# A graph layer with a gated expert mix on one core: the row fix by one-hot products, the last sums stored ahead of the output loads, two of seven tiles mixed on TensorE

## The reference, cut to what matters

```python
x = x + relu(ln(x) @ W + segment_sum((ln(x) @ M)[src], dst))      # 6250 nodes x 256, 200000 edges
xn = ln(x)
h = (xn @ W_gat).reshape(M, 4, 4)                                 # 4 heads x 4 experts
e = leaky_relu(a_src[src] + a_dst[dst], 0.2)                      # 131072 edges, and one loop per node
ee = exp(e - segment_max(e, dst)[dst])
alpha = ee / (segment_sum(ee, dst)[dst] + 1e-16)
scores = layernorm(segment_sum(h[src] * alpha, dst) + b_gat).mean(heads)
w = softmax(top2(scores))                                         # per node, over 4 experts
x = x + sum_e w[:, e] * (gelu(xn @ W1[e] + b1[e]) @ W2[e] + b2[e])
```

## Time and profile before

| | us |
|---|---|
| median of 3 runs | 3240.63 |
| lowest, highest | 3239.18, 3240.84 |
| the profiled execution's own time | 3242.23 |
| its span | 3240.9 |

### The profile page before, as it was taken

How to read it: one execution, slowest core, us unless ns; L and a number is a source line. 1 busy time by engine, 2 the same in 40 slices (tenths; PEclk the granted TensorE clock), 3 DMA queues, 4 the chain that set the end, 5 groups by cost and what they waited for, 6 DMA issues and landing times.

```text
span 3240.9 us, 41199 instructions
## 1 busy us (share of the span) xinstructions
PE 2411.0 (74%) x13096; PEld 1894.9 (58%) x13096; DVE 2192.3 (68%) x5126; ACT 543.2 (17%) x924; POOL 2331.4 (72%) x2315
## 2 busy tenths in 40 slices
PE   1466878878778888788888888886888888888300
PEld 0344555556556555566666666664788887888200
DVE  6488777678685656565556555553588888888568
ACT  4000212112123333211111111111000000000012
POOL 3777777777777777777777777774777777777073
PEclk9777999889889989899999999898999999999655
DMA  8876777667767777777777777774122122211518
GB/s 277 297 226 218 221 224 226 216 214 230 218 208 243 239 223 238 223 223 236 232 247 246 239 235 238 234 237 131 26 62 62 39 61 62 55 44 44 192 43 270
DMA packets 470542, 599.63 MB, mean 185 GB/s; under 512 B 66293, under 2 KB 409270, under 8 KB 468278
## 3 DMA queue, kind: packets, MB, share of 16 engines
q1 hardware_dynamic: 372310, 375.12, 34.9%
q0 software_dynamic: 97568, 220.03, 24.6%
q10 hardware_dynamic: 448, 1.85, 0.2%
HBM read 312.22 MB, written 286.19 MB: 185 GB/s over the span
## 4 chain that ended last, share of the span: by engine, by line
PE 32%; DVE 16%; DMA 9%; issue 6%; POOL 5%; SPq 3%; ACT 1%; DVEq 0%; POOLq 0%; ACTq 0%
PE wide L1266 9%; PE wide L1368 9%; PE wide L1324 5%; PE wide L1314 5%; DMA run_d<-ring 4%; DVE g L871 2%; DMA fetched<-x_d 2%; DVE ring L746 2%; DVE low_hot L788 2%; DVE comb L995 2%; DVE picked L799 2%; PE wide L1283 2%; POOL ring L1438 1%; POOL start_d L1454 1%; DMA ring<-xn_d,srci 1%
## 5 line engine op out<-in xcount | busy, mean ns | idle before, releaser
L1438 POOL DMA_INDIRECT ring<-xn_d,srci x1611 | 1623.4, 1008 | 516.7 <-issue 443.6
L746 DVE SCALAR_TENSOR_TENSOR ring<-ring,same_v,wide 128x256 f32<-128x256 f32 x1610 | 770.6, 479 | 694.8 <-PE wide L1266 588.0
L1266 PE MATMUL wide<-ring,one_hot 128*128 128x256 f32 x3222 | 916.8, 421 | 164.5 <-DVE ring L746 95.1
L1266 PEld LDWEIGHTS wide<-ring,one_hot 128*128 128x128 f32 x3222 | 652.7, 211 | 377.8 <-DVE ring L746 132.6
L1368 PE MATMUL wide<-tab_parts,low_hot 128*128 128x208 bf16 x6144 | 599.9, 263 | 120.2 <-DVE low_hot L788 120.2
L1368 PEld LDWEIGHTS wide<-tab_parts,low_hot 128*128 128x128 bf16 x6144 | 576.4, 102 | 145.5 <-DVE low_hot L788 128.4
L1465 POOL DMA_INDIRECT g<-tab_d,srt x512 | 547.2, 1069 | 156.0 <-issue 154.2
L1324 PE MATMUL wide<-w2s,hh 128*128 128x256 f32 x1568 | 390.1, 394 | 2.3 <-DVE yo L724 2.3
L1314 PE MATMUL wide<-xt,w1s 128*128 128x512 f32 (+1 forms) x832 | 390.8, 594 | 0.8 <-DVE feat L714 0.8
L1324 PEld LDWEIGHTS wide<-w2s,hh 128*128 128x128 f32 x1568 | 311.7, 200 | 56.0 <-issue 6.1
L1079 ACT ACTIVATE hh<-wide,b1c 128x512 f32<-128x512 f32 (+1 forms) x208 | 137.8, 663 | 1218.2 <-PE wide L1314 1217.9
(11 more groups left out here) (332 smaller groups left out, 1569.8 us busy)
## 6 DMA issues: line engine op xcount, KB each, us to landing
run_d<-ring SPq DMA_DIRECT2D x201, 1024.0 KB, 5.3
ring<-xn_d,srci POOLq DMA_INDIRECT x1611
y_d<-yo SPq DMA_DIRECT2D x196, 128.0 KB
comb<-y_d SPq DMA_DIRECT2D x28, 896.0 KB, 9.6
low_row<-low_d SPq DMA_DIRECT2D x16, 1024.0 KB, 5.6
sum_d<-g SPq DMA_DIRECT2D x16, 768.0 KB, 3.3
g<-tab_d,srt POOLq DMA_INDIRECT x512
xn_d<-ring SPq DMA_DIRECT2D x7, 896.0 KB, 5.6
```

The lines of the kernel that those rows point to most:

```text
L746: dve_at["run", j] = step(V.scalar_tensor_tensor(out=o, in0=ring[:, (j - 1) // JC % RING, (j - 1) % JC, :], scalar=same_v[:, j:j + 1], in1 ...
L1266: T.matmul(wide[:, 4 + j // 2 % 2, j % 2 * D:(j % 2 + 1) * D], one_hot[:, j // 4 % 4, j % 4, :], ring[:, j // JC % RING, j % JC, :], start ...
L1438: G.indirect_dma_start(out=ring[:, s, j % JC, :], out_offset=None, in_=xn_d, in_offset=at_rows(srci[:, j:j + 1])).then_inc(sem(f"gather{s} ...
```

## The change

- The row fix is no longer written to `sum_d`. The node gathers follow the gather of the rows to be fixed at once, and fetch the unfixed sums. VectorE builds two one-hot operands in the fix (`node_of`: which node of a tile, `tile_of`: which tile), spreads the fixed row over 49 tiles x 24 values (`fix_r`), and TensorE's four products place the fixed rows: a map of which nodes are replaced, and their values. The gates take `fsum * keep + fix_r`.
- SP stores the last sums before the loads of the output stage.
- `comb` has four slots. The fourth lies over the buffers of the edge stage, so SP waits for these before it loads chunk 3. In the output loop the loads of y no longer wait for the output's store to land; the load of x1 does, one chunk later.
- GpSimd does nothing in the mix. For two of the seven tiles ScalarE makes `diag` (the identity scaled by the weights of one expert, 128x128), TensorE sums x1 and the four experts' rows with five float32 products in a PSUM bank, and ScalarE copies the bank over x1 in `comb`.

The diff, without the moves of the buffers:

```diff
 
-CR = 3
+CR = 4
 PART = 3
-POOL_TILES = 2
+PE_TILES = 2
+DIAGS = 4
...
             row_ends(sm[:, 5:6], row_at[:, 0:1], sm[:, 3:4], sm[:, 4:5], smi[:, 2:3], smi[:, 3:4], "fix_f")
+            then(V.tensor_single_scalar(smi[:, 5:6], smi[:, 4:5], P - 1, ALU.bitwise_and))
+            then(V.tensor_copy(sm[:, 80:81], smi[:, 5:6]))
+            then(V.tensor_single_scalar(smi[:, 5:6], smi[:, 4:5], 7, ALU.logical_shift_right))
+            then(V.tensor_copy(sm[:, 81:82], smi[:, 5:6]))
+            then(V.tensor_scalar(sm[:, 82:83], sm[:, 11:12], -1.0, 1.0, ALU.mult, ALU.add))
...
         then(V.tensor_tensor(cfix[:, HX:FE], bank[2][:, HX:FE], sm[:, 64:68], ALU.mult))
-        dve_at["fix_row"] = then(V.tensor_tensor(sm[:, 32:32 + FE], sm[:, 32:32 + FE], cfix[:, 0:FE], ALU.add))
+        then(V.tensor_tensor(sm[:, 32:32 + FE], sm[:, 32:32 + FE], cfix[:, 0:FE], ALU.add))
+        node_of, tile_of, keep = tmask, smt[:, 0, :], smt[:, 1, :]
+        step(V.tensor_scalar(node_of[:, :], iota_f[:, :], sm[:, 80:81], sm[:, 82:83], ALU.is_equal, ALU.mult))
+        then(V.tensor_scalar(tile_of, iota_f[:, 0:NT], sm[:, 81:82], None, ALU.is_equal))
+        dve_at["fix_rows"] = then(V.tensor_tensor(
+            fix_r[:, :, :], tile_of[:, :, None].broadcast_to([P, NT, FG]),
+            sm[:, None, 32:32 + FG].broadcast_to([P, NT, FG]), ALU.mult))
+        V.wait_ge(sem("rows_fixed"), 1)
+        then(V.tensor_scalar(keep, bank[3][:, 0:NT], -1.0, 1.0, ALU.mult, ALU.add))
+        step(V.tensor_tensor(keep, keep, has_f[:, :], ALU.mult))
+        for i, (a, b) in enumerate(FIX_PARTS):
+            step(V.tensor_copy(fix_r[:, a:b, :], bank[4 + i][:, 0:(b - a) * FG].rearrange("p (t f) -> p t f", f=FG)))
+        step.settle()
...
             a_s, a_d, top_ = ft[:, :, HX:FE], ft[:, :, FE:FG], fs[:, :, FE:FG]
-            then(V.tensor_tensor(fs, fs, hs.broadcast_to([P, n, FG]), ALU.mult))
+            then(V.tensor_tensor(fs, fs, smt[:, 1, t0:t1, None].broadcast_to([P, n, FG]), ALU.mult))
+            then(V.tensor_tensor(fs, fs, fix_r[:, t0:t1, :], ALU.add))
...
 
+        mixed = 0
         for c in range(NLN):
             for part, (t0, t1) in enumerate(PARTS):
                 if c * XG == t0:
                     gate(part, t0, t1)
             s = c % CR
             A.wait_ge(sem(f"comb_in{s}"), 16 * (NX + 1) * (c // CR + 1))
-            for e in range(NX):
-                for k in range(XG - POOL_TILES, XG):
-                    y = comb[:, s, e, k, :]
-                    A.activation(y, y, ACT.Copy, scale=fin[:, 7, c * XG + k, e:e + 1]).then_inc(sem("scaled"), 1)
+            for k in range(XG - PE_TILES, XG):
+                if mixed >= DIAGS:
+                    A.wait_ge(sem("mixed"), mixed - DIAGS + 1)
+                for e in range(NX):
+                    A.activation(diag[:, mixed % DIAGS, e, :], ident[:, :], ACT.Copy,
+                                 scale=fin[:, 7, c * XG + k, e:e + 1]).then_inc(sem("diags"), 1)
+                mixed += 1
+            for k in range(XG - PE_TILES, XG):
+                n = c * PE_TILES + k - (XG - PE_TILES)
+                A.wait_ge(sem("mixed"), n + 1)
+                A.activation(comb[:, s, NX, k, :], bank[4 + n % 4][:, 0:D], ACT.Copy).then_inc(sem("poured"), 1)
...
         mm.then_inc(sem("carried"), 1)
+        T.wait_ge(dve_step, dve_at["fix_rows"])
+        T.matmul(bank[3][:, 0:NT], tmask[:, :], smt[:, 0, :], start=True, stop=True)
+        for i, (a, b) in enumerate(FIX_PARTS):
+            mm = T.matmul(bank[4 + i][:, 0:(b - a) * FG], tmask[:, :], fix_r[:, a:b, :].rearrange("p t f -> p (t f)"),
+                          start=True, stop=True)
+        mm.then_inc(sem("rows_fixed"), 1)
+        T.wait_ge(dve_step, dve_at["gates", 0])
+        for c in range(NLN):
+            s = c % CR
+            T.wait_ge(sem(f"comb_in{s}"), 16 * (NX + 1) * (c // CR + 1))
+            for k in range(XG - PE_TILES, XG):
+                n = c * PE_TILES + k - (XG - PE_TILES)
+                T.wait_ge(sem("diags"), NX * (n + 1))
+                if n >= 4:
+                    T.wait_ge(sem("poured"), n - 3)
+                T.matmul(bank[4 + n % 4][:, 0:D], ident[:, :], comb[:, s, NX, k, :], start=True, stop=False)
+                for e in range(NX):
+                    mm = T.matmul(bank[4 + n % 4][:, 0:D], diag[:, n % DIAGS, e, :], comb[:, s, e, k, :],
+                                  start=False, stop=(e == NX - 1))
+                mm.then_inc(sem("mixed"), 1)
...
                              in_offset=at_rows(smi[:, 2:3])).then_inc(sem("fix_in"), 16)
-        G.wait_ge(dve_step, dve_at["fix_row"])
-        G.indirect_dma_start(out=sum_d, out_offset=at_rows(smi[:, 3:4]), in_=sm[:, 32:32 + FG], in_offset=None,
-                             bounds_check=E2 - 1, oob_is_err=False).then_inc(sem("fix_out"), 16)
-        G.wait_ge(sem("fix_out"), sent(0))
         for part, (t0, t1) in enumerate(PARTS):
             for t in range(t0, t1):
                 G.indirect_dma_start(out=fsum[:, t, :], out_offset=None, in_=sum_d,
                                      in_offset=at_rows(idx_f[:, t:t + 1])).then_inc(sem(f"node_in{part}"), 16)
-        n_scaled, n_added = 0, 0
-        for c in range(NLN):
-            s = c % CR
-            G.wait_ge(sem(f"comb_in{s}"), 16 * (NX + 1) * (c // CR + 1))
-            for e in range(NX):
-                n_scaled += POOL_TILES
-                G.wait_ge(sem("scaled"), n_scaled)
-                if n_added:
-                    G.wait_ge(sem("added"), n_added)
-                for k in range(XG - POOL_TILES, XG):
-                    o = comb[:, s, NX, k, :]
-                    G.tensor_tensor(o, o, comb[:, s, e, k, :], ALU.add).then_inc(sem("added"), 1)
-                n_added += POOL_TILES
...
 
-        def load_comb(c):
-            s = c % CR
-            if c >= CR:
-                Q.wait_ge(sem(f"out{s}"), sent(c // CR - 1))
-            rows_ = slice(c * XG * P, (c + 1) * XG * P)
-            for e in range(NX):
-                Q.dma_start(comb[:, s, e, :, :], y_d[e, rows_, :].rearrange("(t p) d -> p t d", p=P)).then_inc(sem(f"comb_in{s}"), 16)
-            Q.dma_start(comb[:, s, NX, :, :], x1_d[rows_, :].rearrange("(t p) d -> p t d", p=P)).then_inc(sem(f"comb_in{s}"), 16)
-
+        def load_rows(c, e):
+            s, rows_ = c % CR, slice(c * XG * P, (c + 1) * XG * P)
+            Q.dma_start(comb[:, s, e, :, :], (x1_d if e == NX else y_d[e])[rows_, :].rearrange("(t p) d -> p t d", p=P)
+                        ).then_inc(sem(f"comb_in{s}"), 16)
+
+        store_sums(NCF - 1)
         for c in range(CR):
-            load_comb(c)
-        store_sums(NCF - 1)
+            if c == CR - 1:
+                for a in range(NCF - GR, NCF):
+                    Q.wait_ge(sem(f"sum_out{a % GR}"), sent(a // GR))
+                Q.wait_ge(sem("carried"), 1)
+                Q.wait_ge(sem("exps"), NCF)
+                Q.wait_ge(sem("carry_exp"), 1)
+            for e in range(NX + 1):
+                load_rows(c, e)
         for c in range(NLN):
             s = c % CR
             Q.wait_ge(dve_step, dve_at["combined", c])
-            Q.wait_ge(sem("added"), NX * POOL_TILES * (c + 1))
+            Q.wait_ge(sem("poured"), PE_TILES * (c + 1))
             n = min(XG, FULL // P - c * XG)
             Q.dma_start(out[c * XG * P:(c * XG + n) * P, :].rearrange("(t p) d -> p t d", p=P),
                         comb[:, s, NX, 0:n, :]).then_inc(sem(f"out{s}"), 16)
             if n < XG:
                 Q.dma_start(out[FULL:N, :], comb[0:N - FULL, s, NX, n, :]).then_inc(sem(f"out{s}"), 16)
             if c + CR < NLN:
-                load_comb(c + CR)
+                for e in range(NX):
+                    load_rows(c + CR, e)
+            if 1 <= c <= NLN - CR:
+                Q.wait_ge(sem(f"out{(c - 1) % CR}"), sent((c - 1) // CR))
+                load_rows(c - 1 + CR, NX)
```

More of the change, by code:

```diff
@@ L209, in build @@
     q = Region(r4)
+    fix_r = q.take("fix_r", [P, NT, FG], F32)
+    q = Region(q.at - NT * HX * 4)
     fin = q.take("fin", [P, 8, NT, HX], F32)
+    hm = q.take("hm", [P, 2, HEADS, P], F32)
+    fsum = q.take("fsum", [P, NT, FG], F32)
     r.at = max(r.at, q.at)
@@ L257, in build @@
     comb = q.take("comb", [P, CR, NX + 1, XG, D], F32)
-    r.at = max(r.at, q.at)
-    hm = r.take("hm", [P, 2, HEADS, P], F32)
-    fsum = r.take("fsum", [P, NT, FG], F32)
+    diag = q.take("diag", [P, DIAGS, NX, P], F32)
     oc = r.take("oc", [P, 9], F32)
@@ L299, in build @@
     PARTS = ((0, PART * XG), (PART * XG, NT))
+    FIX_PARTS = tuple((a, min(a + 512 // FG, NT)) for a in range(0, NT, 512 // FG))
     ZERO_OUT = 16 * (FS + 1)
@@ L993, in vector_program @@
             for e in range(NX):
-                for k in range(XG - POOL_TILES):
+                for k in range(XG - PE_TILES):
                     step(V.scalar_tensor_tensor(
```

## The result

The changed kernel took 3182.47 us (median of 4 runs, 3180.70 to 3186.38) against 3240.74 us before (median of 4): 58.3 us less, a ratio of 0.9822 with a 95% interval of 0.9806 to 0.9838. The forecast was 3179. The profiled execution took 3180.70 us, the shortest of the four, with a span of 3179.2.

A forecast was written before the change was run, and what follows sets the result against it. It took a chain of waits to bound the last 220 us: gathers first, then loads and VectorE. Sum: 3172.0 + 1.0 + 6.5 = 3179.5 us of span, 61.4 less; median 3240.6 - 61.4 = 3179, range 3168 to 3198.

The forecast's parts named there:

- TensorE's term: Mixes after gate 1: TensorE's two tiles per chunk take 32.9 us against VectorE's 33.6; 1 us added for order.
- Store first: Start of the tail: the last sums, stored ahead of the loads, land in 3.3 us at 3042.3, 28.7 us earlier.
- Fix off the gathers' path: Between the fix row's gather and the first node gather: 1.25 us instead of 7.4, without the write back.
- Landing: Node gathers beside loads: each lands in 5 us, with 2.3 and 7.0 kept, moving the forecast by -2.7 or +2.0.
- the rival of gathers held up behind the loads: Node gathers beside a full SP queue: each takes 10.3 us and POOL waits; end 3255 us, chance 0.03.
- Fix by products: During part 0's gathers: the fix by TensorE's products ends near 3061, 13 us before gate 0, costing nothing.
- Gates and mixes: VectorE's tail: gate 0 18.0 us, gate 1 20.8, each mix 8.4 without GpSimd beside it; mixes end at 3172.0.
- Loads: Output-stage loads: at 348 GB/s, 2.64 us each, they land ahead of their use; VectorE is late last.
- The rival of the loads: Output stage: loads at 301 GB/s take 3.05 us each, chunk 5 starts 6.4 us late; 3185 us, chance 0.14.
- the rival of TensorE at the half clock: After gate 1: four chunks at half clock take 46.4 us and set the end at 3191 us; chance 0.14.
- My 7.1 and 11.6: TensorE's us per chunk of two tiles at full and at half clock, including some 2.1 us idle, against VectorE's 8.4.
- End: From VectorE's last operation to the end of the span, for the last store: 6.5 us, unchanged.

The follow-up runs named there:

- e10: The kernel before with one edit, the last sums stored ahead of the loads: 3219.8 us, ratio 0.994 to the kernel before.
- e2: The changed kernel with the last sums stored after 14 of the loads instead of before them: 3209.2 us, ratio 0.990 to the kernel before.
- e12: The changed kernel with all output-stage loads held until part 0's gathers have landed: 3199.8 us, ratio 0.989 to the kernel before.
- e4: The changed kernel with the row fix written back to device memory before the node gathers: 3200.0 us, ratio 0.987 to the kernel before.
- e3: The changed kernel with the two tiles scaled by ScalarE and added by GpSimd, as before: 3211.9 us, ratio 0.990 to the kernel before.
- e1: The changed kernel with three buffers instead of four, new load order kept: 3199.5 us, ratio 0.987 to the kernel before.
- e11: The kernel before with only the fourth buffer and the output loop's new load order, 14 loads ahead of the store: 3236.8 us, ratio 1.000.

## Why the prediction was right, by its own steps

The forecast of the span was met to 0.3 us (3179.5 against 3179.2), partly by luck; the median missed its forecast by 3.5 us (3182.5 against 3179). Three things came together: the part before the last scan was 2.1 us shorter than in the profile of before, which no edit explains; the profiled execution was the shortest of its four; and the tail was 142.5 us where my steps give 3179.5 - 3038.8 = 140.7. The 1.8 us are the store's landing (+1.2), the gathers' (+0.7), small parts of the gathers, the gates and the end (+0.9), and TensorE's term (-1.0). The medians differ by 58.3 us, not by the 61.4 of the working: the profile of before stood 1.5 us above its median, that of the changed kernel 1.8 below.

- *Store first.* Right in kind; alone it is worth 19.9 us (e10) and undone it costs 21.8 (e2). It landed in 4.5 us, not 3.3: loads follow it here. Without them it takes 3.2 (e12).
- *Fix off the gathers' path.* 1.25 us to the first node gather, as reckoned. Its worth was put too low in one respect: I compared with 7.4 us, but beside loads the write back takes 13.8 (e4), so this edit is worth 10.6 us there.
- *Landing.* 5.7 us for the 5 that I took between 2.3 and 7.0. That a DMA engine serves its queues in turns (the Trainium skill, DMA: Bandwidth & Descriptors, Queues, rings and completion order) agrees with there being no 10.3 us for the gathers, but the turns are not free: e12 gives 2.3 without loads. GpSimd kept its 1.25 us from gather to gather, so the rival of gathers held up behind the loads falls.
- *Fix by products.* Done at 3057.4, 17 us before gate 0 and some 4 us earlier than reckoned; the cover held.
- *Gates and mixes.* 18.2 and 20.8 us against 18.0 and 20.8; 8.4 us for a mix as forecast. The reason, GpSimd's additions, is shown by e3.
- *Loads.* They ran at 332 GB/s beside the gathers (each 5 us from 3045 to 3095), not at 348, and still were ahead of VectorE: e1 and e12, which take slack away, make VectorE wait, and the changed kernel shows no such wait. The rival of the loads falls for the changed kernel.
- *TensorE.* The term of 1 us was wrong: VectorE was last, and TensorE's last tile was copied out at 3165.4, 7 us before VectorE's end; the rival of TensorE at the half clock falls. TensorE ran at the half clock of 1.2 GHz only for about the first tile of each part (granted clock 0.60 in the window of 3095 to 3100 us, 1.00 in the three that follow to 3115), and chunks then came 6.2 us apart, not 7.1: ten products took 4.3 us and the pause 1.7. My 7.1 and 11.6 did not follow from the rows that they name. With the pause of 2.1 us, ten products at 1.10 and 2.05 us a pair make 7.6 and 12.4, which would have put TensorE 1.5 us behind VectorE; in a stream the products are cheaper than these pairs. The Trainium skill (TensorE: Matmul & The Clock Gate, HAM oscillation) tells of bursts that fall back to the slow clock after each wait, with waits longer than these. Inside a part, with pauses of 1.7 us, none did here; over gate 1, where TensorE had nothing for 26.6 us, it began again at half.
- *End.* 6.8 us against 6.5.

The four edits undone one by one cost 9.9, 21.8, 25.3 and 10.6 us, 67.6 together, against 59.6 for the whole: they are not independent. Most of the 8 us shows in one place: the wait for the write back is 12.6 us beside the loads in e4 (13.8 - 1.25) and 6.2 where the queues are idle because the store came late (7.4 - 1.25). The rest is not parted by any run. Done alone the store brings 19.9 and the buffer, with the new order of loads, nothing.

## What to carry to other kernels

In a tail that is one chain, look for what stands in the chain only because of its place in a queue: a small store behind large loads held this one up, and putting it first was worth 20 us alone, while the loads that it delayed by 12 us had slack. Then go through the chain again, because the next thing late decides what the rest is worth: a fourth buffer brought nothing by itself, since its loads made the fix dearer by as much as they saved later beside an engine slowed by its neighbour, and it was worth 10 us once both were gone. A round trip through device memory costs more the fuller the queues are, so price it beside the traffic that will be there, not beside that of the profile.

## What the runs showed of the hardware

From the issue of a row gather, over a small fix on VectorE, to the landing of the 12 KB write that follows it, 13.8 to 15.0 us passed beside loads (e4, e10, e11; 341 to 349 GB/s in e4), twice the 7.4 us of an idle queue. A gather of node sums landed in 5.7 us beside loads at 332 GB/s and in 2.3 without them (e12), while GpSimd's pace of issue stayed at 1.25 us. One addition of 128x256 on GpSimd (every 0.85 us) cost VectorE's operations of the same size 0.45 us, with the transfers at 3 GB/s and at 332 alike (e3).
